# Group 0 of a fused linear layer computed with x stationary, and W1 and W2 loaded over 128 partitions

## The chip, the core and the metric

The kernel runs on one core of a Trainium2 chip. Its time is device time in microseconds, the median of several executions. TensorE multiplies, VectorE (DVE), ScalarE (ACT) and GpSimd (POOL) work on rows in SBUF, and SyncE (SP) issues most of the DMA transfers; ScalarE issues some at the start.

## What is computed

```python
# x (4, 1024, 512), cond (4, 256), W (1536, 512), b (512), all fp32
hidden = concatenate([cond, cond], axis=-1)            # (4, 512)
x_mean = mean(x, axis=1, keepdims=True)                # (4, 1, 512)
fused = concatenate([x, x_mean * ones, hidden * ones], axis=-1)
out = x + relu(einsum('bld,do->blo', fused, W) + b)
```

W falls into W1 (for x), W2 (for the mean) and W3 (for cond), of 512 rows each. The mean and cond parts are the same for all rows of a batch, so they make one bias line for each batch: mean @ W2 + hidden @ W3 + b.

## The kernel before

The 4096 rows of x are 8 groups of 512; two groups make a batch. Only x @ W1 is done for every row. To keep fp32 precision each factor is split in a high part of a shorter float type and a rest (xh and xl, w1h and w1l), and a product takes three matmuls: xh w1h, xl w1h, xh w1l. The inner dimension 512 is four slices k of 128.

In groups 0 to 6 W1 is stationary and x streams: an output tile t (one of four) is 128 output columns by 512 rows, in a PSUM bank of its own (ps_y, four banks). In group 7, the last, x rows are stationary and W1 columns stream (`last_product`), so its output needs no turning back. Group 0 is done in two halves of 256 rows, k outermost, as data arrive.

For a piece of x (one k of one group) VectorE turns it by 32x32 blocks into PSUM (`turn_x`, L331), ScalarE writes xh and adds up the columns for the mean (`x_high`, L257), VectorE subtracts to get xl (`x_low`, L337). x lies in SBUF by quadrants of 32 partitions, one for each 128 columns; a load of a group of x is four transfers of 32 partitions, one a quadrant, with rows of 512 bytes. ScalarE makes w1h (L250), GpSimd w1l (L227). W1 and W2 are loaded by quadrants as well (`load_w1`, `load_w2`), with rows of 2 KB.

Behind a tile, ScalarE adds bias and applies relu (L275), VectorE turns it back (L344), GpSimd adds x (L232), SP stores. The first tiles are complete before their bias is known: ScalarE saves eight of them in relu_t (L262), and applies bias and relu later. The bias of batch b needs both its groups: VectorE forms w2x, the W2 rows weighted by x's sums (`mean_terms`, L356 to L361, 128x512 a step), TensorE adds over partitions (`mean_bias`, L476), VectorE adds the constant part const_row (L411), which comes from cond and W3 (`const_product`, L525), and spreads it (`sum_bias`, L375, L378). The last group takes its bias as a line of rows, stored to DRAM and loaded back (bias_line, last_bias).

Each engine runs its instructions in the order of the code; semaphores alone tie them together. SP's queue is one list: x0, W1, cond, x1, x2, W2, b, x3, W3, x4 to x7, then the last group's x as rows, then the stores. Rows of it stand below, with the change.

Of the kernel before, what the change touches and what calls it, by code (L numbers as in the profile page):

```python
# [37 lines left out]
WARM = 14  # L38


def build(nc, x, cond, w, bvec, out):
# [13 lines left out]
    pieces = [(0, l, HL, k) for l in (0, HL) for k in range(NK)]  # L55
    pieces += [(g, 0, NL, k) for g in range(1, G) for k in range(NK)]

    def pieces_to(g):
        return NK * g + NK * (g > 0 if isinstance(g, int) else 1)
# [24 lines left out]
    bias_line = nc.dram_tensor("bias_line", [D], F32).ap()  # L84
# [7 lines left out]
    with ExitStack() as ctx:  # L92
# [13 lines left out]
        w2x = sb("w2x", [P, D])  # L106
# [10 lines left out]
        xsum = sb("xsum", [P, G + 1, NK])  # L117
# [6 lines left out]
        bias_row = sb("bias_row", [P, P])  # L124
# [53 lines left out]

# [3 lines left out]
        def _(sp):  # L182
# [430 lines left out]
```

## Time and profile before

| | |
|---|---|
| Median of 3 runs | 104.74 us (104.71 to 105.04) |
| Profiled execution, its own time | 105.25 us, of which the span of the core 103.1 us |
| TensorE busy | 97.4 us, 95% of the span |
| VectorE / ScalarE / GpSimd busy | 79% / 46% / 40% |
| DMA | 21.39 MB, mean 207 GB/s |

The durations come from the profiled execution. It has 2.15 us around the span, and is 0.5 us above the median. Matmuls are pipelined, so the time from one start to the next is what a product costs, not the duration in its row. The profile counts a DMA packet for each contiguous run that an engine moves, and small packets of 4 bytes that signal completion.

### The profile page before, as it was taken

How to read it: one execution, taken by the hardware profiler on the slowest of the kernel's cores; microseconds unless marked ns; L12 is line 12 of the kernel's file. 1: busy time of each engine (PE TensorE's matmuls, PEld its weight loads, DVE VectorE, ACT ScalarE, POOL GpSimd, SP SyncE). 2: the span in 40 equal slices, each digit the busy share in tenths (PEclk: the TensorE clock that was granted, in tenths of full speed). 3: DMA queues.
4: the chain of work that ended last, by engine and by line, in shares of the span. 5: the costliest groups of instructions: out<-in, count | busy, mean ns of one | idle time of the engine just before them, and what ended most of it. 6: DMA issues, size and time to landing. Idle time of an engine off the chain costs nothing.

```text
span 103.1 us, 1694 instructions
## 1 busy us (share of the span) xinstructions
PE 97.4 (95%) x523; PEld 78.3 (76%) x523; DVE 81.7 (79%) x146; ACT 47.3 (46%) x116; POOL 41.0 (40%) x37
## 2 busy tenths in 40 slices
PE   5989999999999898999999999999999999999970
PEld 2349999778888585888888886888888886888960
DVE  3173869979879999999999994999999994839660
ACT  3277426875606549777487100874744004610000
POOL 1029700000000000999857700468577059992000
PEclk9999999999999999999999999999999999999997
DMA  2999999999999999999999999300591690199995
GB/s 63 290 306 273 220 214 216 235 235 218 233 270 253 209 224 221 225 225 224 219 296 349 309 282 251 97 0 0 111 267 29 144 253 14 39 279 263 230 330 183
DMA packets 34990, 21.39 MB, mean 207 GB/s; under 512 B 1572, under 2 KB 32680, under 8 KB 34984
## 3 DMA queue, kind: packets, MB, share of 16 engines
q1 hardware_dynamic: 33400, 20.13, 85.4%
q10 hardware_dynamic: 1584, 1.18, 3.8%
q8 instruction: 3, 0.05, 0.2%
q14 instruction: 3, 0.02, 0.1%
HBM read 12.91 MB, written 8.39 MB: 207 GB/s over the span
## 4 chain that ended last, share of the span: by engine, by line
PE 57%; SPq 18%; DMA 10%; DVE 7%; issue 3%; ACT 1%; DVEq 0%
PE ps_y L457 46%; DMA xa<-in_x_dram 10%; SPq L162 9%; PE ps_y L558 4%; PE ps_y L560 4%; PE ps_y L559 4%; SPq L166 2%; SPq L170 2%; DVE w2x L361 2%; DVE ps_xt L331 2%; SPq L158 2%; SPq L195 2%; ACT xh L257 1%; DVE xl L337 1%; SPq L190 1%
## 5 line engine op out<-in xcount | busy, mean ns | idle before, releaser
L232 POOL TENSOR_TENSOR xa<-xa,back 128x512 f32 x28 | 35.6, 1295 | 45.8 <-DVE back L344 45.8
L457 PE MATMUL ps_y<-xh,w1h 128*128 (+2 forms) x128 | 43.7, 368 | 0.3 <-ACT w1h L250 0.3
L457 PE MATMUL ps_y<-xl,w1h 128*128 (+2 forms) x128 | 43.1, 363 | 0.0
L457 PE MATMUL ps_y<-xh,w1l 128*128 (+2 forms) x128 | 42.9, 363 | 0.0
L257 ACT ACTIVATE xh<-ps_xt 128x512 fp32r<-128x512 f32 (+1 forms) x36 | 19.7, 549 | 21.1 <-DVE ps_xt L331 21.1
L331 DVE STREAM_TRANSPOSE ps_xt<-xa 128x512 f32<-128x512 f32 (+1 forms) x36 | 22.3, 643 | 5.8 <-DMA xa<-in_x_dram 5.4
L457 PEld LDWEIGHTS ps_y<-xh,w1h 128*128 128x128 f32 x128 | 22.6, 188 | 5.6 <-issue 0.8
L457 PEld LDWEIGHTS ps_y<-xh,w1l 128*128 128x128 f32 x128 | 22.6, 189 | 3.9
L337 DVE TENSOR_TENSOR xl<-ps_xt,xh 128x512 fp32r<-128x512 f32 (+1 forms) x36 | 22.2, 618 | 4.1 <-ACT xh L257 4.1
L457 PEld LDWEIGHTS ps_y<-xl,w1h 128*128 128x128 f32 x128 | 22.7, 189 | 3.5
L275 ACT ACTIVATE relu_t<-ps_y,bias 128x512 f32<-128x512 f32 x20 | 13.5, 686 | 16.5 <-DVE bias L378 15.0
L344 DVE STREAM_TRANSPOSE back<-relu_t 128x512 f32<-128x512 f32 x28 | 18.6, 685 | 1.1 <-ACT relu_t L275 1.1
L361 DVE SCALAR_TENSOR_TENSOR w2x<-w,bsum,w2x 128x512 f32<-128x512 f32 x12 | 9.0, 751 | 0.4
L227 POOL TENSOR_TENSOR w1l<-w,w1h 128x512 fp32r<-128x512 f32 x4 | 5.1, 1304 | 6.2 <-ACT w1h L250 6.2
L257 ACT ACTIVATION_READ_ACCUMULATOR xh<-ps_xt 128x1 f32 x36 | 7.1, 196 | 0.0
L558 PE MATMUL ps_y<-w1h,xh 128*128 128x512 f32 (+1 forms) x20 | 6.9, 347 | 0.0
L559 PE MATMUL ps_y<-w1l,xh 128*128 128x512 f32 (+1 forms) x20 | 6.9, 346 | 0.0
L560 PE MATMUL ps_y<-w1h,xl 128*128 128x512 f32 (+1 forms) x20 | 6.9, 345 | 0.0
L454 PE MATMUL ps_mean<-warm 128*128 128x512 bf16 x14 | 5.6, 587 | 1.2 <-DVE warm L390 1.2
L275 ACT ACTIVATE relu_t<-relu_t,bias 128x512 f32<-128x512 f32 x8 | 5.0, 710 | 1.7 <-DVE bias L378 1.7
L454 PEld LDWEIGHTS ps_mean<-warm 128*128 128x128 bf16 x14 | 1.9, 141 | 4.4 <-issue 3.2
L262 ACT ACTIVATE relu_t<-ps_y 128x512 f32<-128x512 f32 x8 | 4.5, 596 | 1.2 <-PE ps_y L457 1.2
(34 smaller groups left out, 35.8 us busy)
## 6 DMA issues: line engine op xcount, KB each, us to landing
xa<-in_x_dram SPq DMA_DIRECT2D x28, 256.0 KB, 7.2
out_dram<-xa SPq DMA_DIRECT2D x28, 256.0 KB, 4.1
w<-in_L_cond_W_dram SPq DMA_DIRECT2D x4, 256.0 KB, 7.6
w<-in_L_cond_W_dram SPq DMA_DIRECT2D x2, 512.0 KB, 8.3
w<-in_x_dram SPq DMA_DIRECT2D x4, 256.0 KB, 6.2
out_dram<-w SPq DMA_DIRECT2D x3, 256.0 KB, 3.2
xa<-in_x_dram SPq DMA_DIRECT2D x4, 128.0 KB, 3.6
xa<-in_x_dram ACTq DMA_DIRECT2D x4, 128.0 KB, 4.0
```

What stands on the lines that cost most here:

```text
L162: eng.dma_start(xa[Q * j:Q * j + Q, g], xv[g, j]).then_inc(x_landed[g], 16)
L232: nc.gpsimd.tensor_tensor(rows, rows, back[:, t], ALU.add).then_inc(added, 1)
L257: nc.scalar.activation(xh[:, g % SLOTS, k, l:l + nl], ps_xt[:, n % XT_BANKS, 0:nl], ACT.Copy, accum_out=xsum[:, part, k:k + 1]).then_inc(x ...
L275: nc.scalar.activation(relu_t[:, slot], products, ACT.Relu, bias=bias[:, g // H, t, g // H:g // H + 1]).then_inc(relu_done, 1)
L331: nc.vector.transpose(ps_xt[:, n % XT_BANKS, 0:nl], xa[:, g, l // Q:(l + nl) // Q, Q * k:Q * k + Q]).then_inc(xt_ready, 1)
L337: nc.vector.tensor_tensor(xl[:, g % SLOTS, k, l:l + nl], ps_xt[:, n % XT_BANKS, 0:nl], xh[:, g % SLOTS, k, l:l + nl], ALU.subtract).then_i ...
L344: nc.vector.transpose(back[:, n % BACK_RING], relu_t[:, n % RELU_RING].rearrange("p (lb om) -> p lb om", om=Q)).then_inc(turned_back, 1)
L361: nc.vector.scalar_tensor_tensor(out=w2x[:], in0=w2[:, k], scalar=bsum[:, k:k + 1], in1=w2x[:], op0=ALU.mult, op1=ALU.add).then_inc(w2x_st ...
L457: return nc.tensor.matmul(ps_y[:, t, ls], lhs, rhs, start=start, stop=stop, skip_group_check=True)
L558: nc.tensor.matmul(y, xh[:, slot, k, rows], cols_h, start=start, stop=False, skip_group_check=True)
L559: nc.tensor.matmul(y, xh[:, slot, k, rows], cols_l, start=False, stop=False, skip_group_check=True)
L560: return nc.tensor.matmul(y, xl[:, slot, k, rows], cols_h, start=False, stop=stop, skip_group_check=True)
```

## The change

Group 0 is computed as group 7 is: x rows stationary (128 a tile), W1 columns streaming, 512 wide. Its x comes in three parts, of 128, 128 and 256 rows, and its first 24 products (tiles r = 0, 1) need parts one and two. Its tiles leave PSUM as rows: ScalarE copies them into w1's place (`save_first`), GpSimd adds the bias line there, ScalarE applies relu, GpSimd adds x rows, which are loaded a second time into group 0's place in xa; SP stores them after group 3. The bias line of batch 0 goes through DRAM for that, between the loads of x5, x6 and x7.

W1 is loaded slice by slice over 128 partitions (slice 0 in two transfers of 64 partitions, one from SP and one from ScalarE), W2 in four transfers of 128. VectorE makes half of each slice of w1h. cond is loaded behind x1. VectorE forms batch 1's sums ahead of its wait for W3's product, into a second half of w2x, and TensorE does the mean products of odd batches in ps_const's bank; those of batches 0 and 1 stand in the third and the last tile of group 2. Six tiles are saved for a later relu, not eight. The loops over groups on TensorE and GpSimd are written out. The warm-up has 10 matmuls, not 14.

```diff
-WARM = 14
+WARM = 10
-    pieces = [(0, l, HL, k) for l in (0, HL) for k in range(NK)]
+    PARTS = ((0, P), (P, P), (2 * P, 2 * P))
+    FIRST = ((0, 0), (0, 1), (0, 2), (1, 0), (1, 1), (0, 3), (1, 2), (1, 3)) + tuple((2, k) for k in range(NK))
+    pieces = [(0, *PARTS[part], k) for part, k in FIRST]
...
-        def load_w1(eng, first, end, quadrants):
-            for j in quadrants:
-                eng.dma_start(w1[Q * j:Q * j + Q, first:end], wv[0, j, :, first:end]).then_inc(w1_landed[first], 16)
-
-        def load_w2(eng, quadrants):
-            for j in quadrants:
-                eng.dma_start(w2[Q * j:Q * j + Q], wv[1, j]).then_inc(w2_landed, 16)
+        def load_w1(eng, k, first, end):
+
+            eng.dma_start(w1[Q * first:Q * end, k], wv[0, first:end, :, k]).then_inc(w1_landed[k], 16)
+
+        def load_w2(eng, k):
+            eng.dma_start(w2[:, k], wv[1, :, :, k]).then_inc(w2_landed, 16)
...
+            load_x(sp, 4, ORDER)
+            load_x(sp, 5, ORDER)
+
+            sp.wait_ge(bias_summed, 1)
+            for j in range(NQ):
+                sp.dma_start(bias_line[0, P * j:P * j + P], bias_row[Q * j, 0]).then_inc(bias_stored, 16)
+            load_x(sp, 6, ORDER)
+            sp.wait_ge(bias_stored, 16 * NQ)
+            sp.dma_start(last_bias[:], bias_line[0].partition_broadcast(P)).then_inc(last_bias_landed, 16)
+            load_x(sp, 7, ORDER)
...
+            for n, (g, t) in enumerate(tiles):
+                residual(g, t, n + 1)
+                r = n - BIAS_FROM
+                if 0 <= r < NR:
+
+                    pool.wait_ge(y_free, r + 1)
+                    pool.wait_ge(last_bias_landed, 16)
+                    nc.gpsimd.tensor_tensor(first_y[:, r], first_y[:, r], last_bias[:], ALU.add).then_inc(first_biased, 1)
+                r = n - X0_FROM
+                if 0 <= r < NR:
+
+                    pool.wait_ge(first_relu_done, r + 1)
+                    pool.wait_ge(first_x_landed, 16 * NR)
+                    nc.gpsimd.tensor_tensor(first_x[:, r], first_x[:, r], first_y[:, r], ALU.add).then_inc(first_added, 1)
...
             turn_x(n_x)
             turn_and_split(n_x, n_x + NK)
+            mean_terms(1)
             dve.wait_ge(const_summed, 1)
             dve.wait_ge(b_landed, 16 * NQ)
             nc.vector.tensor_tensor(const_row[:], ps_const[:, 0:P], b_row[:], ALU.add).then_inc(const_ready, 1)
             dve.wait_ge(const_ready, 1)
             sum_bias(0)
-            mean_terms(1)
+            sum_bias(1)
...
+            def first_rows(k, r, x, w, start=False, stop=False):
+
+                return nc.tensor.matmul(ps_y[:, r], x[:, 0, k, P * r:P * r + P], w[:, k], start=start, stop=stop, skip_group_check=True)
```

`wv` is W1 and W2 seen as (s, j, m, k, o), row 128 j + 32 k + m of each: `wv[0, j, :, 0]` is 32 rows one after another, `wv[1, :, :, k]` is 4 blocks of 32 rows, the blocks 128 rows apart.

SP's queue from its start, before; names are target<-source, then partitions x elements, and how many. One DMA row is one kind of transfer (w is w1, w2 or w3 here; ScalarE's queue issues as many of x0 and W1 beside it).

```order
L158 DMA xa<-in_x_dram 32x8x128 x2
L166 DMA w<-in_L_cond_W_dram 32x512 x4
L166 DMA w<-in_L_cond_W_dram 32x2x512 x2
L158 DMA xa<-in_x_dram 32x8x128 x2
L190 DMA cond_c<-in_cond_dram 4x64 [waits cond_zeroed]
L190 DMA cond_c<-in_cond_dram 4x64 x3
L162 DMA xa<-in_x_dram 32x16x128 x8
L170 DMA w<-in_L_cond_W_dram 32x4x512 x4
L195 DMA b_row<-in_L_cond_b_dram 32x128 x4
L162 DMA xa<-in_x_dram 32x16x128 x4
```

The same place in the changed kernel:

```order
L171 DMA xa<-in_x_dram 32x4x128 x2
L179 DMA w<-in_L_cond_W_dram 64x1x512
L171 DMA xa<-in_x_dram 32x4x128 x2
L179 DMA w<-in_L_cond_W_dram 128x1x512 x3
L171 DMA xa<-in_x_dram 32x8x128 x4
L175 DMA xa<-in_x_dram 32x16x128 x4
L211 DMA cond_c<-in_cond_dram 4x64 [waits cond_zeroed]
L211 DMA cond_c<-in_cond_dram 4x64 x3
L175 DMA xa<-in_x_dram 32x16x128 x4
L182 DMA w<-in_L_cond_W_dram 128x1x512 x4
L216 DMA b_row<-in_L_cond_b_dram 32x128 x4
L175 DMA xa<-in_x_dram 32x16x128 x4
```

The W1 and W2 transfers cover 64 or 128 partitions in place of 32, and are fewer; x0 comes in three parts, cond stands behind x1.

VectorE behind the turning of group 3's pieces, before: last splits, constant row, bias 0, sums of batch 1, first tiles turned back.

```order
L337 TENSOR_TENSOR xl<-ps_xt,xh 128x512 [waits xh_ready] x2
L411 TENSOR_TENSOR const_row<-ps_const,b_row 128x128 [waits b_landed,const_summed]
L375 SCALAR_TENSOR_TENSOR bias_row<-ps_mean,const_row 128x128 [waits mean_done,const_ready]
L378 STREAM_TRANSPOSE bias<-bias_row 128x128 [waits bias_summed]
L356 TENSOR_TENSOR bsum<-xsum 128x4 [waits w2x_step,mean_done]
L358 TENSOR_SCALAR w2x<-w,bsum 128x512 [waits bsum_ready]
L361 SCALAR_TENSOR_TENSOR w2x<-w,bsum,w2x 128x512 [waits w2x_step] x3
L344 STREAM_TRANSPOSE back<-relu_t 128x512 [waits relu_done] x2
```

And in the changed kernel:

```order
L407 TENSOR_TENSOR xl<-ps_xt,xh 128x512 [waits xh_ready] x2
L436 TENSOR_TENSOR bsum<-xsum 128x4 [waits w2x_step]
L438 TENSOR_SCALAR w2x<-w,bsum 128x512 [waits bsum_ready]
L441 SCALAR_TENSOR_TENSOR w2x<-w,bsum,w2x 128x512 [waits w2x_step] x3
L517 TENSOR_TENSOR const_row<-ps_const,b_row 128x128 [waits b_landed,const_summed]
L456 SCALAR_TENSOR_TENSOR bias_row<-ps_mean,const_row 128x128 [waits mean_done,const_ready]
L459 STREAM_TRANSPOSE bias<-bias_row 128x128 [waits bias_summed]
L456 SCALAR_TENSOR_TENSOR bias_row<-ps_const,const_row 128x128 [waits mean_done]
L459 STREAM_TRANSPOSE bias<-bias_row 128x128 [waits bias_summed]
L417 STREAM_TRANSPOSE back<-relu_t 128x512 [waits relu_done]
```

The five rows of sums of batch 1 have moved ahead of the wait for const_summed; the first turn back stands behind both biases.

## Rows read from the trace of the kernel before

**Rows 1.** The page: span, and part 1 (busy time and share of the span, instructions).

```profile
span 103.1 us, 1694 instructions
PE 97.4 (95%) x523; PEld 78.3 (76%) x523; DVE 81.7 (79%) x146; ACT 47.3 (46%) x116; POOL 41.0 (40%) x37
```

**Rows 2.** TensorE's timeline: start, us, what, count [idle before, what ended it].

```profile
1.19 5.61 PE L454 MATMUL ps_mean<-warm 128*128 128x512 bf16 x14 [1.19 <-DVE warm L390]
7.07 0.71 PE L457 MATMUL ps_y<-xh,w1h 128*128 128x256 f32 x4 [0.27 <-ACT w1h L250]
...
18.53 0.28 PE L457 MATMUL ps_y<-xh,w1l 128*128 128x256 f32 x1
18.65 0.40 PE L457 MATMUL ps_y<-xh,w1h 128*128 128x512 f32 x1
...
33.66 0.39 PE L457 MATMUL ps_y<-xh,w1l 128*128 128x512 f32 x1
34.52 1.08 PE L525 MATMUL ps_const<-w,cond_t 128*32 128x128 f32 x32 [0.47 <-DMA w<-in_L_cond_W_dram]
...
39.78 0.39 PE L457 MATMUL ps_y<-xh,w1l 128*128 128x512 f32 x1
40.57 0.43 PE L476 MATMUL ps_mean<-w2x,ones 128*32 128x128 f32 x8 [0.40 <-DVE w2x L361]
40.93 0.50 PE L457 MATMUL ps_y<-xh,w1h 128*128 128x512 f32 x1
```

**Rows 3.** The chain that ended last, in order of time: start, us, what.

```profile
36.54 0.29 DVE const_row L411
...
37.42 0.13 DVE bsum L356
...
39.67 0.76 DVE w2x L361
...
41.00 22.01 PE ps_y L457 x96
```

**Rows 4.** The DMA queues from 86.0 to 88.4 us.

```profile
DMA packets 9, 0.01 MB, mean 4 GB/s; under 512 B 4, under 2 KB 8, under 8 KB 8
q1 hardware_dynamic: 8, 0.00, 0.4%
...
bias_line<-bias_row SPq DMA_DIRECT2D x4, 0.5 KB
```

**Rows 5.** The page, DMA packets of the whole span.

```profile
DMA packets 34990, 21.39 MB, mean 207 GB/s; under 512 B 1572, under 2 KB 32680, under 8 KB 34984
```

**Rows 6.** Four stretches: engines' busy time, granted clock, share of DMA engines, GB/s.

```profile
core 0: us, PE busy (x) PEld busy (x) DVE busy (x) ACT busy (x) POOL busy (x), PEclk, DMA share, GB/s
5.00:6.50 1.50, 1.50 (x6) 0.55 (x4) 0.90 (x3) 0.93 (x5) 0.00 (x0) 1.00 1.02 337
7.80:9.80 2.00, 2.00 (x19) 2.00 (x19) 0.77 (x2) 1.65 (x6) 2.00 (x3) 1.00 1.20 292
11.00:14.50 3.50, 3.50 (x32) 3.50 (x31) 2.84 (x8) 1.79 (x8) 1.14 (x1) 1.00 1.21 217
51.80:54.20 2.40, 2.40 (x12) 2.01 (x11) 2.24 (x5) 2.17 (x6) 1.11 (x1) 1.00 1.05 308
```

**Rows 7.** The DMA queues from 100.2 us to the end, in 40 slices.

```profile
GB/s 396 395 396 339 396 452 382 438 353 325 325 353 339 396 339 353 367 339 269 241 226 170 226 169 99 28 28 28 14 14 0 0 0 0 0 0 0 0 0 0
```

**Rows 8.** The timelines of VectorE, ScalarE and GpSimd.

```profile
4.69 0.79 DVE L331 STREAM_TRANSPOSE ps_xt<-xa 128x256 f32<-128x256 f32 x2 [2.89 <-DMA xa<-in_x_dram]
6.30 0.63 ACT L250 ACTIVATE w1h<-w 128x512 fp32r<-128x512 f32 x1
7.09 5.05 POOL L227 TENSOR_TENSOR w1l<-w,w1h 128x512 fp32r<-128x512 f32 x4 [6.20 <-ACT w1h L250]
...
30.91 1.32 DVE L331 STREAM_TRANSPOSE ps_xt<-xa 128x512 f32<-128x512 f32 x2 [0.65 <-DMA xa<-in_x_dram]
...
37.59 5.02 ACT L275 ACTIVATE relu_t<-relu_t,bias 128x512 f32<-128x512 f32 x8 [1.69 <-DVE bias L378]
```

More of the change, by code:

```diff
@@ L105, in build @@
         w3 = sb("w3", [P, 2, CK, D])
-        w2x = sb("w2x", [P, D])
+        w2x = sb("w2x", [P, 2, D])
         ones = sb("ones", [P, Q])
@@ L203, in _ @@
                 sp.dma_start(last_x[:, r], x_rows[LAST, :, r]).then_inc(last_x_landed, 16)
-            for g in range(LAST):
+            for g in range(1, LAST):
                 if g == LAST - 2:
@@ L472, in mean_bias @@
             def mean_bias(b):
+                if b == 1:
+                    pe.wait_ge(const_ready, 1)
+                elif b > 1:
+                    pe.wait_ge(bias_ready, b - 1)
                 pe.wait_ge(w2x_step, NK * b + NK)
                 for j in range(NQ):
-                    last = nc.tensor.matmul(ps_mean[Q * j:Q * j + Q, 0:P], ones[:, 0:Q], w2x[:, P * j:P * j + P], start=True, stop=True)
+                    last = nc.tensor.matmul(mean_bank(b)[Q * j:Q * j + Q, 0:P], ones[:, 0:Q], w2x[:, b % 2, P * j:P * j + P], start=True, stop=True)
@@ new lines, in _ @@
+            for k in range(NK):
+                pe.wait_ge(w1h_ready, k + 1)
+                pe.wait_ge(w1h_rest_ready, k + 1)
+                for r in (0, 1):
+                    piece = FIRST.index((r, k))
+                    pe.wait_ge(xh_ready, piece + 1)
+                    first_rows(k, r, xh, w1h, start=(k == 0))
+                    pe.wait_ge(xl_ready, piece + 1)
+                    first_rows(k, r, xl, w1h)
+                if k == 0:
+                    first_low(0)
+                elif k > 1:
+                    first_low(k - 1)
@@ new lines, in _ @@
+            first_low(NK - 1, stop=True)
+            for k in range(NK):
+                piece = FIRST.index((2, k))
+                pe.wait_ge(xh_ready, piece + 1)
+                if k == NK - 1:
+                    pe.wait_ge(xl_ready, piece + 1)
+                    for r in (2, 3):
+                        first_rows(k, r, xh, w1h)
+                        first_rows(k, r, xl, w1h)
+                        first_rows(k, r, xh, w1l, stop=True).then_inc(y_ready, 1)
+                    break
+                for r in (2, 3):
+                    first_rows(k, r, xh, w1h, start=(k == 0))
+                pe.wait_ge(xl_ready, piece + 1)
+                for r in (2, 3):
+                    first_rows(k, r, xl, w1h)
+                    first_rows(k, r, xh, w1l)
@@ L516, in _ @@
+            pe.wait_ge(y_free, 2)
+            for k in range(NK):
+                pe.wait_ge(xl_ready, pieces_to(1) + k + 1)
+                for t in (0, 1):
+                    last = product(1, k, t)
+                    if k == NK - 1:
+                        last.then_inc(y_ready, 1)
+            for t in (2, 3):
+                pe.wait_ge(y_free, t + 1)
                 tile(1, 1, t)
```

322 lines of the change are left out of this document (183 added, 139 removed).

## The prediction

> **What bounds the kernel now.** I read the page's busy shares first [rows 1]: TensorE is busy 95% of a span of 103.1 us, so the time is TensorE's first product, its work, and its gaps. Its own timeline gives these [rows 2]. Products start at 7.07 us, as w1h becomes ready; group 0 runs to 18.65 us without a gap. From there a 512-column product comes every 0.227 us (33.66 in the row is the last before a stop). Two stops follow, both in group 2. The one ahead of the constant products: 33.66 + 0.23 = 33.89 to 34.52, 0.63 us, for W3. The one ahead of batch 1's mean product: 39.78 + 0.23 = 40.01 to 40.57, 0.56 us, for w2x. From 41.00 the chain that ended last is TensorE's products, 96 of them in one piece of 22.01 us [rows 3].
>
> The chain also shows what set 40.57 [rows 3]. VectorE can start on group 3's x at 30.91, after 0.65 us of waiting for its DMA [rows 8]; I call that the landing. VectorE turns and splits its four pieces, reaches const_row at 36.54, and makes batch 1's w2x from 37.42 to 39.67 + 0.76 = 40.43. So behind group 3's x stand 5.7 us of splitting, then constant and bias, then 3.0 us of sums. Before it in the load queue stand x0 (1 MB), W1 (1 MB), x1, x2, W2: what stretches the loads stretches the kernel.
>
> **How many DMA engines a transfer uses.** This decides the case, and two counts of packets show it. In 86.0 to 88.4 us four transfers of one row store bias_row [rows 4]. The queue has 8 packets, 4 of them under 512 bytes: one data packet and one small completion packet each. Every engine that takes part leaves one completion packet, so each of these used one engine. The whole page has 1572 packets under 512 bytes [rows 5]. The program issues 96 transfers whose outermost count is 32 or 128 on both sides, 4 of cond with outermost count 4 (rows of 256 bytes), and 4 of bias_row with 1. With sixteen engines for the first kind, four for cond, one for bias_row: 96 x 16 + 4 x (4 + 4) + 4 x 1 = 1536 + 32 + 4 = 1572, to the packet. Were cond and bias_row to signal from sixteen engines, it would be 1536 + 80 + 64 = 1680. So a count of 4 outermost means four engines.
>
> The Trainium skill says the same in general: in "DMA: Bandwidth & Descriptors", on why a DMA increments its semaphore by 16, the hardware generator takes the largest number up to 16 that divides the slowest count of source and of destination, and the lowest-numbered engines. By that rule the new W loads, 4 at the source and 128 at the destination, get four engines, and the time is that of my first case below; were it not to hold, it would be that of the second. Trace and rule agree for the counts 1 and 4; no transfer of before has different counts on its two sides, so no run here shows that case yet.
>
> **The change, part by part.**
>
> *W1 and W2 over 128 partitions.* The destination counts 128 partitions, but the source is walked as (j, m, o): outermost 4 with a stride of 128 rows, then 32. For W1's first slice each of two transfers has outermost 2 at the source, 64 at the destination. The unseen price is what happens when the sides differ. Bounds: the destination decides, sixteen engines; or the smaller count decides, four and two engines. I take the smaller: both counts seen so far were obeyed, and a split by outermost index can't make sixteen parts of four.
>
> Then engine 0 carries, ahead of group 3's x: half of slice 0 (64 rows of 2 KB over the two queues), a quarter of slices 1 to 3 (96 rows), a quarter of W2 (128 rows): 288 rows. Beside these its sixteenth of four groups of x, 256 KB or 512 packets of 512 bytes. Rates per engine, from the windows [rows 6]: the W1 stretch moves 337 GB/s, 21 GB/s an engine, 97 ns a row. The x stretch of 7.8 to 9.8 moves 292, 18.3 an engine, 28 ns a packet; from 11.0 on x moves at 217, 13.6 an engine, 38 ns. The start of flow: x0's first half is in at 4.69 [rows 8], 0.52 MB at 292 GB/s is 1.8 us, so 2.9. Middle case: 2.9 + 288 x 0.091 + 512 x 0.028 = 2.9 + 26.2 + 14.3 = 43.4 us for group 3's x, against 30.9. Here 0.091 lies between those 97 ns and the 83 ns of the fastest stretch there is, the last stores at 396 GB/s, 24.8 an engine [rows 7]; few engines share the memory, so I lean to neither. Lower bound 2.9 + 288 x 0.083 + 14.3 = 41.1; upper, with W at 97 ns and x at 38, 2.9 + 27.9 + 19.5 = 50.3.
>
> The start: slice 0 is in at 2.9 + 0.9 (x's first 128 rows) + 64 x 0.091 = 9.6, and w1h's half 0.4 later: first product about 10.0 instead of 7.07. Slice 3 is in at 9.6 + 0.9 + 96 x 0.091 = 19.2, its w1l 0.4 + 1.3 later (GpSimd needs 5.05 us for four [rows 8]), so rows 0 and 1 of group 0 end near 21.3 where all of group 0 ended at 18.65. The rest of x0 is in at 21.0; VectorE and ScalarE need some 5 us for its pieces and the two copies between them, so group 0 ends near 27.3, group 1 near 39, and TensorE comes to batch 1's mean product near 50.
>
> *Products 512 wide.* Group 0 had 96 products of 256 columns in 18.65 - 7.07 = 11.58 us; now 48 of 512 at 0.227, 10.9 us. A saving of 0.7 us of TensorE that only counts if it isn't waiting.
>
> *Batch 1's sums ahead of W3, its mean product in the middle of the last tile.* At the same landing L of group 3's x: const_ready is L + 5.7 + 3.0 + 0.35 = L + 9.1; then mean product 0.36 and its restart 0.11, then six products 1.36: group 3 starts at L + 11.0. Before, it started at 40.93 + 0.11 + 12 x 0.227 = 43.8, L + 12.9. This part is worth 1.9 us. const_product, a tile later than before, then doesn't wait for W3 (34.52 before).
>
> *Group 0's own path* (copies to w1's place, four adds of bias and four of x on GpSimd, four relu on ScalarE, 1 MB more loads): hidden. GpSimd works 1.3 us a tile where TensorE needs 2.75, and is idle most of the second half; if bias 0 were late on its line, GpSimd's adds would hold turned_back, and ScalarE's relu behind it. Relu is the near thing: before, eight saved tiles took 5.02 us from 37.59 [rows 8]; now six are saved, and three x steps stand among their relus, each behind VectorE's turn of that piece, so bank 2 comes free some 6.4 us after bias_ready (const_ready + 0.65). TensorE wants it 5.45 us after group 3's start (const_ready + 1.9): 7.05 against 7.35, a margin of 0.3 us. Without it TensorE would wait by as much as relu is late. The shorter warm-up costs nothing where it ends (1.19 + 10 x 0.43 = 5.5) before any product could start. TensorE then idles from 5.5 to 10, and its products may run at the warm-up's pace for a while (0.43 us per 512 columns, the 1.2 GHz level, against 0.227 later): 11 or 12 of group 0's products so slowed are 2.4 us. TensorE has about that to spare, since it comes to the mean product near 50 and const_ready stands at 43.4 + 9.1 = 52.5, so this too is put at nothing; its upper end, 1 us, lies inside the range.
>
> *The loop written out* costs no time that a row shows.
>
> **Sum.** L moves 43.4 - 30.9 = +12.5, the order gives -1.9: +10.6 us on 105.25 us of the profiled execution (0.5 above the median), so 115.8; on the median 104.74, 115.3. After group 3's start nothing changes the 56 us left.
>
> **The rivals.**
> (1) Forecast: W on two and four engines, 0.63. L = 41.1 gives 104.74 + 10.2 - 1.9 = 113.0, L = 50.3 gives 122.2. Its own range is 112.5 to 121: x at 38 ns all the way is what sixteen busy engines get, and most of them will stand idle. For it speak the packet counts; against it, that no row shows a transfer whose sides differ.
> (2) The other side: W over sixteen engines, 0.30. For it: the destination has 128 partitions, and a sixteen-fold split of it is possible. Against: the source has no sixteenth. Then slice 0 is in before 5 us, products start at about 5.5, group 0 ends near 17.7, and the order's 1.9 us is gained, with up to 0.4 more if W2, at 308 instead of 217 GB/s, lets group 3's x come 1.4 us sooner (VectorE is busy with batch 0's sums until 30.91 - 0.65 = 30.3): 102.4 to 102.9, I say 102.7. It decides against me as soon as slice 0 lands before 6 us.
> (3) Sixteen engines, but the relu margin or the bias line on the load queue fails, 0.07: bank 2 late by 1 to 2 us, or x6 behind the wait on bias_summed; 103.5 to 106.
>
> **Numbers.** Less than 0.3% is no change that a measurement of this kernel can tell. Slower: 0.63 of (1) and 0.02 of (3); same 0.03; faster 0.30 + 0.02. Since cases on both sides hold 93% of the chance, the range has to take in both: 102.3 to 120; beside it the likeliest one's own, 112.5 to 121.
>
> **What would show it.** The page's packets under 512 bytes: each W transfer that uses four engines leaves 12 completion packets fewer. ScalarE's first wait for W1 ends at 9 to 10 us (right) or before 5 (wrong). VectorE's first turn of group 3 at 41 to 50 or at 29 to 31. A wait of TensorE ahead of batch 1's mean product; group 3 starting 11.0 us after that turn. If relu's margin fails, TensorE waits for ScalarE 5.5 us into group 3. The forecast is wrong above all if sides that differ are split by the destination.

## The result

Side by side, the kernel before takes 104.89 us (median of 4 runs, 104.71 to 105.09) and the changed kernel 125.34 us (4 runs, 124.95 to 125.73): a ratio of 1.196, interval 1.193 to 1.200. That is slower, as the forecast's likeliest case said, but by 20.5 us instead of 10.6, and beyond the range. The profiled execution took 125.53 us, its span 123.7. Some executions of any of these kernels fall into a slower state, and every median and ratio here and below leaves them out.

The page of the changed kernel: span and busy shares, the granted clock in 40 slices of 3.1 us, and the packets.

```profile
span 123.7 us, 1487 instructions
PE 101.3 (82%) x471; PEld 78.4 (63%) x471; DVE 84.3 (68%) x155; ACT 48.0 (39%) x126; POOL 46.1 (37%) x41
...
PEclk9995559999999999555899999999999999999999
...
DMA packets 34024, 22.71 MB, mean 184 GB/s; under 512 B 1497, under 2 KB 30561, under 8 KB 34017
```

TensorE works hardly longer than before (101.3 against 97.4 us busy), but in a span 20.6 us longer [rows 1]; its granted clock falls twice to half (1.2 GHz), from 9 to 19 us and from 50 to 60; in the page of before no such slice stands. The packets settle the number of engines. With sixteen engines for every W transfer (first experiment below) a page of this program has 1720 packets under 512 bytes. Taking away the 16 completions of each of its 16 W transfers, and adding 2 x 2 for the two-engine transfers and 7 x 4 for the others, gives 1720 - 256 + 32 = 1496; the page has 1497. So W1 and W2 went over two and four engines.

VectorE's timeline, the instructions that waited for a load (start, us, what, in brackets the idle time before and the load): three slices of w1h, x0's second half, x1, batch 0's sums behind W2, and group 3's x.

```profile
12.43 0.29 DVE L479 CAST w1h<-w 128x256 fp32r<-128x256 f32 x1 [8.33 <-DMA w<-in_L_cond_W_dram]
...
17.76 0.29 DVE L479 CAST w1h<-w 128x256 fp32r<-128x256 f32 x1 [0.78 <-DMA w<-in_L_cond_W_dram]
...
21.41 0.29 DVE L479 CAST w1h<-w 128x256 fp32r<-128x256 f32 x1 [3.16 <-DMA w<-in_L_cond_W_dram]
...
22.92 0.79 DVE L401 STREAM_TRANSPOSE ps_xt<-xa 128x256 f32<-128x256 f32 x2 [1.02 <-DMA xa<-in_x_dram]
...
27.26 1.32 DVE L401 STREAM_TRANSPOSE ps_xt<-xa 128x512 f32<-128x512 f32 x2 [0.60 <-DMA xa<-in_x_dram]
...
44.17 0.17 DVE L436 TENSOR_TENSOR bsum<-xsum 128x4 f32<-128x4 f32 x1 [5.18 <-DMA w<-in_L_cond_W_dram]
...
50.15 1.32 DVE L401 STREAM_TRANSPOSE ps_xt<-xa 128x512 f32<-128x512 f32 x2 [2.93 <-DMA xa<-in_x_dram]
```

Group 3's x can be turned at 50.15 against 30.91 before [rows 8]: 19.2 us later. Four stretches of the changed kernel show how the loads run:

```profile
core 0: us, PE busy (x) PEld busy (x) DVE busy (x) ACT busy (x) POOL busy (x), PEclk, DMA share, GB/s
5.00:12.00 7.00, 0.55 (x2) 0.00 (x0) 0.00 (x0) 0.00 (x0) 0.00 (x0) 0.77 0.33 109
12.00:20.00 8.00, 6.03 (x15) 4.42 (x16) 3.96 (x16) 3.44 (x17) 3.83 (x3) 0.56 0.54 160
32.00:45.00 13.00, 13.00 (x59) 10.77 (x58) 7.13 (x16) 5.03 (x14) 0.00 (x0) 1.00 0.53 151
45.00:54.50 9.50, 2.56 (x12) 1.78 (x10) 6.27 (x10) 2.50 (x8) 0.00 (x0) 0.75 1.06 218
```

From 5 to 20 us only a third to a half of the engines' time is used, and 0.53 while W2 comes in (32 to 45), where the stretches read from before have 1.02 to 1.21 at 217 to 337 GB/s [rows 6]. TensorE's timeline shows the price:

```profile
1.19 4.37 PE L561 MATMUL ps_mean<-warm 128*128 128x512 bf16 x10 [1.19 <-DVE warm L471]
...
12.90 0.79 PE L593 MATMUL ps_y<-w1h,xh 128*128 128x512 f32 x1 [7.35 <-ACT w1h L297]
...
47.17 0.39 PE L564 MATMUL ps_y<-xh,w1l 128*128 128x512 f32 x1
54.66 1.94 PE L655 MATMUL ps_const<-w,cond_t 128*32 128x128 f32 x32 [7.10 <-DMA w<-in_L_cond_W_dram]
56.33 0.69 PE L587 MATMUL ps_mean<-w2x,ones 128*32 128x128 f32 x8
56.95 0.79 PE L564 MATMUL ps_y<-xh,w1h 128*128 128x512 f32 x1
...
61.27 0.43 PE L587 MATMUL ps_const<-w2x,ones 128*32 128x128 f32 x8
...
83.22 0.43 PE L587 MATMUL ps_mean<-w2x,ones 128*32 128x128 f32 x8 [0.20 <-DVE w2x L441]
...
87.14 0.50 PE L564 MATMUL ps_y<-xh,w1h 128*128 128x512 f32 x1 [1.24 <-ACT relu_t L330]
```

The first product is at 12.90 (7.07 before [rows 2]). Group 3 starts 1.8 us after the mean product at 61.27, at 63.1, against 43.8. Two more waits, 0.20 us at 83.22 and 1.24 at 87.14, were not in the forecast. VectorE's sums, for batch 1 (w2x in 2.8 us) and for batch 2 (w2x in 4.7 us):

```profile
55.78 0.15 DVE L436 TENSOR_TENSOR bsum<-xsum 128x4 f32<-128x4 f32 x1
55.97 0.49 DVE L438 TENSOR_SCALAR w2x<-w,bsum 128x512 f32<-128x512 f32 x1
56.49 2.33 DVE L441 SCALAR_TENSOR_TENSOR w2x<-w,bsum,w2x 128x512 f32<-128x512 f32 x3
58.74 0.28 DVE L517 TENSOR_TENSOR const_row<-ps_const,b_row 128x128 f32<-128x128 f32 x1
...
77.18 1.09 DVE L436 TENSOR_TENSOR bsum<-xsum 128x4 f32<-128x4 f32 x1
78.31 1.47 DVE L438 TENSOR_SCALAR w2x<-w,bsum 128x512 f32<-128x512 f32 x1
79.82 3.25 DVE L441 SCALAR_TENSOR_TENSOR w2x<-w,bsum,w2x 128x512 f32<-128x512 f32 x3
```

### The profile page after: what moved, and what is told of

It reads as the page before. It is cut to its first block, busy times and chain, and to the rows that moved or that the text cites. A ratio compares the mean times of both kernels' runs of the same rounds, so it can differ in the third digit from the quotient of the medians.

```text
span 123.7 us, 1487 instructions
## 1 busy us (share of the span) xinstructions
PE 101.3 (82%) x471; PEld 78.4 (63%) x471; DVE 84.3 (68%) x155; ACT 48.0 (39%) x126; POOL 46.1 (37%) x41
## 2 busy tenths in 40 slices
DMA packets 34024, 22.71 MB, mean 184 GB/s; under 512 B 1497, under 2 KB 30561, under 8 KB 34017
## 4 chain that ended last, share of the span: by engine, by line
SPq 34%; PE 33%; DVE 16%; DMA 8%; issue 4%; ACT 1%; DVEq 0%; ACTq 0%
PE ps_y L564 22%; SPq L175 13%; DMA w<-in_L_cond_W_dram 8%; SPq L171 8%; DVE xl L407 4%; SPq L216 4%; DVE ps_xt L401 4%; DVE back L417 4%; SPq L179 3%; SPq L182 3%; PE ps_y L688 3%; PE ps_y L690 3%; PE ps_y L689 3%; DVE w2x L441 2%; PE ps_const L655 2%
## 5 line engine op out<-in xcount | busy, mean ns | idle before, releaser
L270 POOL TENSOR_TENSOR xa<-xa,back 128x512 f32<-128x512 f32 x24 | 30.6, 1292 | 50.4 <-DVE back L417 50.3
L564 PE MATMUL ps_y<-xh,w1h 128*128 128x512 f32 x96 | 38.7, 403 | 1.2 <-ACT relu_t L330 1.2
L564 PE MATMUL ps_y<-xl,w1h 128*128 128x512 f32 x96 | 37.9, 395 | 0.0
L564 PE MATMUL ps_y<-xh,w1l 128*128 128x512 f32 x96 | 37.8, 394 | 0.0
L304 ACT ACTIVATE xh<-ps_xt 128x512 fp32r<-128x512 f32 (+2 forms) x40 | 20.5, 512 | 32.8 <-DVE ps_xt L401 32.6
L401 DVE STREAM_TRANSPOSE ps_xt<-xa 128x512 f32<-128x512 f32 (+2 forms) x40 | 23.0, 596 | 7.7 <-DMA xa<-in_x_dram 7.3
L407 DVE TENSOR_TENSOR xl<-ps_xt,xh 128x512 fp32r<-128x512 f32 (+2 forms) x40 | 22.7, 569 | 2.4 <-ACT xh L304 2.4
L564 PEld LDWEIGHTS ps_y<-xh,w1l 128*128 128x128 f32 x96 | 18.3, 191 | 3.9
L330 ACT ACTIVATE relu_t<-ps_y,bias 128x512 f32<-128x512 f32 x18 | 12.2, 690 | 10.4 <-DVE bias L459 9.5
L593 PE MATMUL ps_y<-w1h,xh 128*128 128x512 f32 x16 | 7.4, 492 | 9.9 <-ACT w1h L297 8.8
L593 PE MATMUL ps_y<-w1h,xl 128*128 128x512 f32 x16 | 7.2, 451 | 0.0
```

Of the source, the lines that this page charges most:

```text
L270: nc.gpsimd.tensor_tensor(rows, rows, back[:, t], ALU.add).then_inc(added, 1)
L304: nc.scalar.activation(xh[:, g % SLOTS, k, l:l + nl], ps_xt[:, n % XT_BANKS, 0:nl], ACT.Copy, accum_out=xsum[:, part, k:k + 1]).then_inc(x ...
L330: nc.scalar.activation(relu_t[:, slot], products, ACT.Relu, bias=bias[:, g // H, t, g // H:g // H + 1]).then_inc(relu_done if n < SAVED el ...
L401: nc.vector.transpose(ps_xt[:, n % XT_BANKS, 0:nl], xa[:, g, l // Q:(l + nl) // Q, Q * k:Q * k + Q]).then_inc(xt_ready, 1)
L407: nc.vector.tensor_tensor(xl[:, g % SLOTS, k, l:l + nl], ps_xt[:, n % XT_BANKS, 0:nl], xh[:, g % SLOTS, k, l:l + nl], ALU.subtract).then_i ...
L564: return nc.tensor.matmul(ps_y[:, t, ls], lhs, rhs, start=start, stop=stop, skip_group_check=True)
```

## The experiments

All times are medians, ratios are against the kernel before on the same chip, with a 95% interval. The chips differ from experiment to experiment, so small differences between experiments are best read from the ratios.

### 1. W by quadrants in the changed kernel (e1)

```diff
-            eng.dma_start(w1[Q * first:Q * end, k], wv[0, first:end, :, k]).then_inc(w1_landed[k], 16)
+            for j in quadrants:
+                eng.dma_start(w1[Q * j:Q * j + Q, first:end], wv[0, j, :, first:end]).then_inc(w1_landed[first], 16)
...
-            eng.dma_start(w2[:, k], wv[1, :, :, k]).then_inc(w2_landed, 16)
+            eng.dma_start(w2[Q * j:Q * j + Q], wv[1, j]).then_inc(w2_landed, 16)
```

The calls and wait counts change with them; slices 2 and 3 come in one transfer for each quadrant, and from slice 1 on all are handed out by SP.

> The changed kernel, with W1 and W2 loaded again by quadrants of 32 partitions (outermost count 32 on both sides); all else as changed. Theory A (the narrow W transfers are the whole loss): packets under 512 bytes go back to sixteen completion packets a transfer, first product near 5.5 us, group 0 ends by 18 us, x of group 3 is in at 30 to 31 us, time 102.4 to 103.5 us. Theory B (part of the 20 us comes from the rest of the change: group 0's path on GpSimd and ScalarE, relu's margin, batch 2's bias): time stays above 105 us.

Measured: 106.27 us (105.81 to 106.77), ratio 1.011 (1.004 to 1.017). So the shape of the W loads is 19.1 of the 20.5 us, and the rest of the change loses 1.2 us where it should have gained 2. VectorE's timeline of this run, its first slice of w1h, x1, group 3's x, and then batch 2's sums:

```profile
4.74 0.29 DVE L479 CAST w1h<-w 128x256 fp32r<-128x256 f32 x1 [0.68 <-DMA w<-in_L_cond_W_dram]
...
17.03 1.32 DVE L401 STREAM_TRANSPOSE ps_xt<-xa 128x512 f32<-128x512 f32 x2 [0.88 <-DMA xa<-in_x_dram]
...
32.28 1.32 DVE L401 STREAM_TRANSPOSE ps_xt<-xa 128x512 f32<-128x512 f32 x2 [0.37 <-DMA xa<-in_x_dram]
...
57.91 1.08 DVE L436 TENSOR_TENSOR bsum<-xsum 128x4 f32<-128x4 f32 x1
59.03 1.48 DVE L438 TENSOR_SCALAR w2x<-w,bsum 128x512 f32<-128x512 f32 x1
60.54 3.24 DVE L441 SCALAR_TENSOR_TENSOR w2x<-w,bsum,w2x 128x512 f32<-128x512 f32 x3
```

The first slice is in at 4.74 instead of 12.43, group 3's x at 32.28 instead of 50.15 (30.91 before: this version hands the quadrants out one after another). Group 3 starts at 43.25, 0.5 us earlier than before. But TensorE then stops twice where the kernel before doesn't:

```profile
63.93 0.43 PE L587 MATMUL ps_mean<-w2x,ones 128*32 128x128 f32 x8 [0.79 <-DVE w2x L441]
...
67.85 0.50 PE L564 MATMUL ps_y<-xh,w1h 128*128 128x512 f32 x1 [1.24 <-ACT relu_t L330]
```

Behind both stands VectorE's sum for batch 2, 5.8 us from 57.91 on, while in the kernel before it took 0.99, 0.48 and 2.32 us for the same three rows. What GpSimd does at that time, group 0's bias adds (L279) between the residual adds (L270):

```profile
57.66 1.31 POOL L279 TENSOR_TENSOR w<-w,last_bias 128x512 f32<-128x512 f32 x1
58.92 1.31 POOL L270 TENSOR_TENSOR xa<-xa,back 128x512 f32<-128x512 f32 x1
60.16 1.50 POOL L279 TENSOR_TENSOR w<-w,last_bias 128x512 f32<-128x512 f32 x1
```

### 2 to 4. Only W1, only W2, and the W loads alone in the kernel before (e2, e3, e4)

e2 has e1's first piece of the diff, e3 its second, and e4 is the kernel before with the changed kernel's W loads:

```diff
+        def load_w1(eng, k, first, end):
+            eng.dma_start(w1[Q * first:Q * end, k], wv[0, first:end, :, k]).then_inc(w1_landed[k], 16)
...
+        def load_w2(eng, k):
+            eng.dma_start(w2[:, k], wv[1, :, :, k]).then_inc(w2_landed, 16)
```

> The changed kernel, with W1 alone by quadrants; W2 still in four transfers with outermost count 4 at the source. Theory A: W2 puts 128 rows of 2 KB on each of four engines where 32 fell on each of sixteen; at the 105 ns a row that the changed kernel showed for it this is 13.4 us in place of 4.7, so x of group 3 is in near 39 to 40 us, and the time is 111 to 114 us. Theory B (W1 carries the loss, W2 hides behind products): below 106 us.

> The changed kernel, with W2 alone by quadrants; W1 still narrow. Theory A: first product near 13 us and group 0's end near 29.6 us stay; x of group 3 is in near 41 us, const_row near 50; TensorE, 11 us late from group 0 on, comes to batch 1's mean product near 50 as well, so the time is 114 to 117 us. Theory B (the W3 and W2 waits carry the loss): below 110 us.

> The kernel before with the W1 and W2 loads of the changed one and nothing else. Theory A: it is slow by about what the changed kernel loses and what the rest of it gains, so 125 to 129 us. Theory B: under 120 us.

Measured: e2, with W1 by quadrants, 114.05 us (1.084, 1.075 to 1.093); e3, with W2 by quadrants, 116.07 (1.104, 1.098 to 1.109); e4, with nothing changed but the loads, 124.76 (1.183, 1.174 to 1.192). Each is what its theory A said, to 0.3 us. Against e1 the narrow W2 costs 7.8 us, the narrow W1 9.8, together 17.6 of the 19.1: they nearly add up. e4 is only 0.6 us below the changed kernel, so the rest of the change gained nothing beside the narrow loads. The count of packets under 512 bytes in e4 is 1348, which is 1572 - 256 + 32 to the packet.

### 5 and 6. GpSimd's adds for group 0 later; W1 on two queues ahead of x0's second part (e5, e6)

e5 is e1 with

```diff
-    BIAS_FROM, RELU_FROM, X0_FROM = 4, 9, 9
+    BIAS_FROM, RELU_FROM, X0_FROM = 8, 14, 16
...
-                if g == LAST - 4:
+                if g == LAST - 2:
```

> The run with W1 and W2 by quadrants again, with three numbers changed: GpSimd adds the bias line to group 0's rows after tiles 8 to 11 (was 4 to 7), ScalarE's relus follow from tile 14 (was 9), GpSimd's adds of x0 from tile 16 (was 9), and group 0's rows are stored after group 5 (was 3). Theory A, GpSimd's adds of two arrays from SBUF hold up VectorE's sums for batch 2: those took 5.8 us there (bsum 1.08, w2x 1.48 and 3.24) beside GpSimd's adds and 3.8 us in the kernel before (0.99, 0.48, 2.32) with one add beside them. They shrink to at most 3.9 us, mean_bias(2) waits for nothing, the wait for batch 2's bias at group 5's start falls from 1.4 us to under 0.3, and the time from 106.27 to 104.0 to 104.8. Rival B, the order of the sums' steps on VectorE makes them late whatever GpSimd does: the sums keep over 5 us or the waits stay, and the time is within 0.5 us of 106.27.

Measured: 109.61 us (109.58 to 111.08), 1.056 (1.040 to 1.072). The mechanism was right and the time wrong. VectorE's sums for batch 2 fall to 3.7 us:

```profile
57.41 0.88 DVE L436 TENSOR_TENSOR bsum<-xsum 128x4 f32<-128x4 f32 x1
58.33 0.48 DVE L438 TENSOR_SCALAR w2x<-w,bsum 128x512 f32<-128x512 f32 x1
58.85 2.32 DVE L441 SCALAR_TENSOR_TENSOR w2x<-w,bsum,w2x 128x512 f32<-128x512 f32 x3
```

TensorE runs from group 1 to the end without a wait, its mean product for batch 3 at 84.7 instead of 87.1. But GpSimd's adds of x0 now stand among the last groups' adds, and its last four begin at 91.31:

```profile
81.32 1.29 POOL L270 TENSOR_TENSOR xa<-xa,back 128x512 f32<-128x512 f32 x1 [3.60 <-DVE back L417]
...
91.31 5.94 POOL L270 TENSOR_TENSOR xa<-xa,back 128x512 f32<-128x512 f32 x4
```

They end at 97.25; the stores of group 6 go out behind them, and the last store lands at 107.0. A second chain is as long as TensorE's: VectorE's turns, GpSimd's last adds, the last nine stores.

e6 is e5 with

```diff
+            load_w1(sp, 1, 2, LOW)
+            load_w1(sp, 2, NK, LOW)
             load_x0(sp, 1, LOW)
...
-            load_w1(sp, 1, 2, ORDER)
-            load_w1(sp, 2, NK, ORDER)
...
+            load_w1(act, 1, 2, HIGH)
+            load_w1(act, 2, NK, HIGH)
```

> The run before this one in the list, and every slice of W1 handed out on two queues at once, quadrants 0 and 1 on SP and 2 and 3 on ACT, ahead of group 0's second part, as the kernel before does. Theory A, the serial hand-out was why everything landed 1.4 us later than before (x3 at 32.3 against 30.9): x3 lands by 31.2, group 3 starts near 42.0 (before 43.8), and the time is 102.3 to 103.6, under the kernel before. Rival B, the loads are bound by the bytes: x3 lands at 32 or later and the time is within 0.4 us of the run before this one.

Measured: 112.21 us, 1.077 (1.067 to 1.088). Both were wrong. Group 3's x is in at 29.8, earlier than in the kernel before, as theory A had it, but x0's second part, now behind all of W1, is in only at 8.73 (VectorE waits 1.97 us for it) and holds group 0 back: TensorE stands 2.55 us ahead of 9.51 and works at half clock to 14.7, so batch 1's mean product comes 3.0 us later than in e5. Whether the four transfers that ScalarE hands out in addition also cost time, this run doesn't separate.

### 7 to 9. What put group 3's start 13.0 us behind its x, not 11.0 (e7, e8, e9)

All three are the changed kernel with one edit each.

```diff
-                    elif t == 2 and k == NK // 2:
+                    elif t == 3 and k == 1:
                         const_product()
                         mean_bias(0)
```

> The changed kernel with narrow W loads, and the product of cond and W3 with batch 0's mean product moved from tile 2 of group 2 (k = 2) to tile 3 (k = 1). Theory A, W3's landing (54.5) came last ahead of group 3, 2 us behind the chain of x3's landing: TensorE does 9 products more before it waits, group 3 starts 1.5 to 2.2 us earlier (from 63.1 to about 61.1) and the time falls from 125.3 to 123.1 to 123.8. Rival B, the chain behind x3 alone sets group 3's start: the time stays within 0.4 us of 125.3.

```diff
-WARM = 10
+WARM = 44
```

> The changed kernel with 44 warm-up matmuls in the place of 10, so that TensorE is busy up to the first product at 12.9. Theory A, the half clock of the first products (0.427 us each from 12.9 to 19) is hidden, since the third and fourth slices of W1 land at 17.7 and 21.4 and group 0's end hangs on the fourth: the first products take 0.22 us, group 0 ends within 0.5 us of 29.6, and the time is within 0.4 us of 125.3. Rival B, the missing warm-up costs what its slow products cost: 1 to 2.5 us faster than 125.3.

```diff
+                for _n in range(33):
+                    nc.tensor.matmul(ps_mean[:], warm[:, 0:P], warm[:], start=True, stop=True)
                 pe.wait_ge(cond_spread, 1)
                 pe.wait_ge(w3_landed, 16 * 2)
```

> The changed kernel with narrow W loads, and 33 idle matmuls of 0.21 us ahead of TensorE's wait for W3 (they do no part of the computation), so that TensorE does not stand still for the 7.3 us ahead of the product of cond and W3. Theory A, after the wait it is the half clock (0.427 us a product, 54.7 to 60) that puts group 3's start 2 us behind what the chain from x3's landing allows: group 3 starts at 60.6 to 61.4 (was 63.1) and the time is 123.0 to 124.0. Rival B, the clock is nothing and W3's landing is what came last: the start stays at 63 and the time within 0.5 us of 125.3.

Measured: e7 124.02 us, ratio 1.192 (1.178 to 1.206); e8 124.77, 1.194 (1.182 to 1.207); e9 123.76, 1.179 (1.172 to 1.186). e7 and e8 miss their theory A's range by 0.2 us, e9 lies in it; no rival B is met. In e8 the first products take 0.23 us and batch 1's mean product comes at 61.39 as it did at 61.27: the slow start is hidden, and the 0.6 us that it is below 125.3 lies within the spread of its runs (124.2 to 126.0). In e7 TensorE has 9 products less to do after the wait, and const_row ends the wait of batch 1's mean product at 58.12. Group 3 starts at 61.44, and its x could be turned at 49.21: 12.2 us behind it instead of 13.0, since the six products between still take 0.43 us each. In e9, TensorE's mean products for batches 0 and 1:

```profile
54.73 0.40 PE L587 MATMUL ps_mean<-w2x,ones 128*32 128x128 f32 x8
...
58.09 0.43 PE L587 MATMUL ps_const<-w2x,ones 128*32 128x128 f32 x8
```

With the idle matmuls the products between take 0.23 us (granted clock 1.00 from 53.8 to 60, where the changed kernel has 0.50 from 54.6 to 60), and group 3 starts at 59.94, 10.8 us behind the turn of its x (49.16), as the prediction's own sum had it (11.0). Of the 3.2 us by which it starts earlier 1.0 are the load's, and 2.2 come with the clock. TensorE's last product comes 2.4 us earlier (118.23 against 120.63) and not 3.2, since batch 2's mean product then waits 1.00 us for its sums instead of 0.20; the median falls by 1.6. So the clock alone accounts for all that group 3 was late against the sum, with the products still behind W3. e7, at the low clock, has 0.7 us of it back. The two gains overlap and aren't to be added.

### 10 to 12. GpSimd's adds spread; slice 1 on two queues; the sums put back (e10, e11, e12)

e10 is e1 with

```diff
-    BIAS_FROM, RELU_FROM, X0_FROM = 4, 9, 9
+    BIAS_AT, RELU_AT, X0_AT = (4, 5, 8, 9), (10, 11, 12, 13), (10, 11, 12, 13)
```

e11 is e10 with

```diff
-            load_w1(sp, 1, 2, ORDER)
+            load_w1(sp, 1, 2, LOW)
...
             load_x0(act, 1, HIGH)
+            load_w1(act, 1, 2, HIGH)
```

and e12 is e10 with

```diff
-            mean_terms(1)
             dve.wait_ge(const_summed, 1)
...
             sum_bias(0)
-            sum_bias(1)
+            mean_terms(1)
...
+                if n == 1:
+                    sum_bias(1)
...
+                            if g == H + 1 and k == 3:
+                                mean_bias(1)
```

> The run with W1 and W2 by quadrants, with GpSimd's bias adds for group 0 after tiles 4, 5, 8 and 9 (were 4 to 7), and ScalarE's relus and GpSimd's adds of x0 after tiles 10 to 13 (were 9 to 12), so that fewer of GpSimd's adds stand beside VectorE's sums for batch 2; group 0's rows are stored after group 3 again. Theory A, with the sums at under 4.8 us TensorE waits for nothing between group 1's start and the last group, as in the run with all adds later, and the stores aren't pushed to the end: 103.3 to 104.4, 1.9 to 2.9 us below 106.27. Rival B, whatever moves GpSimd's adds later ends in later stores: 105.5 or more.

> The run before this one in the list, with slice 1 of W1 handed out on two queues (quadrants 2 and 3 on ScalarE's, behind group 0's second part). Theory A, TensorE is the bound and its start decides: slice 1 and those behind it land about 1 us earlier, TensorE's stops in group 0 (1.3 us at slice 2) shrink by 0.5 to 1 us, and the time is 0.3 to 1.0 us under the run before. Rival B, ScalarE's two more hand-outs delay its first high half and the first product by 0.9 us: within 0.3 us of the run before, or slower.

> The run with GpSimd's adds spread (second in the list), with batch 1's sums put back behind batch 0's: VectorE makes them after batch 0's bias, TensorE's mean product for batch 1 stands in group 3's first tile (k = 3), and its bias is summed after the turn of tile 0. Theory A, with group 0's own path the relu that needs batch 1's bias comes two tiles later, and TensorE is continuous either way: within 0.4 us of the run with GpSimd's adds spread. Rival B, the step of the prediction, group 3 waits for the sums: 1.5 to 2.2 us slower than it.

Measured: e10 106.47 us, 1.014 (1.007 to 1.020); e11 104.90, 0.999 (0.993 to 1.005); e12 106.93, 1.019 (1.013 to 1.024). e10 has batch 3's mean product 2 us earlier than e1 (85.2 against 87.1) and is no faster: rival B's time. Its sums for batch 3 now stand beside GpSimd's moved adds and take 5.4 us (e5's take 3.5), and GpSimd's last add ends at 94.84, as e1's does at 94.94:

```profile
78.17 2.63 DVE L436 TENSOR_TENSOR bsum<-xsum 128x4 f32<-128x4 f32 x1
...
84.38 10.46 POOL L270 TENSOR_TENSOR xa<-xa,back 128x512 f32<-128x512 f32 x8 [3.60 <-DVE back L417]
```

e11 is 1.6 us below e10, more than theory A's 0.3 to 1.0, and level with the kernel before. e12 is 0.5 us above e10, with intervals that overlap, near theory A's 0.4 and far from rival B's 1.5 to 2.2: with group 0's rows out of the chain of relus, batch 1's sums can stand early or late. In e11 all eight residual adds of the last two groups run back to back:

```profile
82.70 10.47 POOL L270 TENSOR_TENSOR xa<-xa,back 128x512 f32<-128x512 f32 x8 [2.82 <-DVE back L418]
```

### 13. Without GpSimd's eight adds for group 0 (e13)

e11 with both adds of GpSimd for group 0 taken out, and the waits on them turned to ScalarE's relu and the loads.

```diff
-                    nc.gpsimd.tensor_tensor(first_y[:, r], first_y[:, r], last_bias[:], ALU.add).then_inc(first_biased, 1)
...
-                    nc.gpsimd.tensor_tensor(first_x[:, r], first_x[:, r], first_y[:, r], ALU.add).then_inc(first_added, 1)
```

> The run with slice 1 of W1 on two queues and GpSimd's adds spread, with GpSimd's eight adds for group 0 left out (its rows are stored without bias and without x0; the loads, ScalarE's relus and the stores stay). Theory A, what the faster loads and the sums ahead of W3 gain is eaten by GpSimd's eight more adds (10.4 us of them), beside VectorE's sums for batches 2 and 3 and ahead of the last eight adds of the groups, behind which the last stores stand: VectorE's sums take 3.8 us and less, GpSimd's last add ends 1 to 2 us earlier than 93.2, and the time is 102.3 to 103.8. Rival B, the end is bound by TensorE and the stores alone: within 0.5 us of 104.9.

Measured: 103.57 us (103.15 to 104.54), 0.985 (0.980 to 0.991). Theory A's time: 1.3 us below e11. The sums take 3.7 us for batches 2 and 3. GpSimd's last adds in its profiled execution come in two pieces with a rest between, no longer one block:

```profile
82.35 5.01 POOL L271 TENSOR_TENSOR xa<-xa,back 128x512 f32<-128x512 f32 x4 [3.60 <-DVE back L408]
87.96 5.04 POOL L271 TENSOR_TENSOR xa<-xa,back 128x512 f32<-128x512 f32 x4 [0.60 <-DVE back L408]
```

The end of the last add, 93.0, is no earlier than e11's 93.2, in an execution that was 1 us above its median; that piece of the expectation isn't borne out by this trace, and neither does it show where the 1.3 us were saved (TensorE's last product is at 99.42, e11's at 98.29).

### 14. The moved sums alone, in the kernel before (e14)

```diff
+            mean_terms(1)
             dve.wait_ge(const_summed, 1)
...
-            mean_terms(1)
+            sum_bias(1)
...
-                    elif t == 1 and k == NK // 2:
+                    elif t == 2 and k == NK // 2:
                         const_product()
                         mean_bias(0)
+                    elif t == 3 and k == NK // 2:
+                        mean_bias(1)
```

> The kernel before with one part of the change alone: the sums for batch 1 ahead of W3's product (a second half of w2x, batch 1's mean product in the bank of the product of cond and W3), the product of cond and W3 in tile 2 of group 2 and batch 1's mean product in tile 3. Theory A, TensorE's two stops there are all there is to gain (0.86 us ahead of the product of cond and W3 at 34.52 and 0.79 at 40.57, less 0.2 to 0.3 that such a step takes without a wait): group 3 starts 0.9 to 1.2 us earlier than 43.8, and 0.5 to 1.2 us of it is left in the time. Rival B, the step of the prediction: 1.9 us less. Rival C, the last stores and GpSimd's last adds set the end: within 0.3 us of before.

Measured: 108.81 us (107.85 to 109.44), 1.040 (1.036 to 1.044): slower, against all three. TensorE is ready for group 3 at 43.5, and then waits for a free bank. ScalarE's relus of the eight saved tiles, and TensorE's wait:

```profile
40.16 5.02 ACT L283 ACTIVATE relu_t<-relu_t,bias 128x512 f32<-128x512 f32 x8 [4.65 <-DVE bias L389]
```

```profile
46.16 0.49 PE L467 MATMUL ps_y<-xh,w1h 128*128 x1 [2.52 <-ACT relu_t L283]
```

Batch 0's bias is now made behind batch 1's sums, so these relus begin at 40.16 instead of 37.59 [rows 8] and take 5.02 us; the bank of group 3's first tile is free one relu behind them. So group 3 starts 2.4 us later than before; the runs lie 2.9 to 4.5 us above before's median, and what the rest of that is, I can't name. With group 0 out of that queue of relus (e10 against e12) the moved sums cost nothing: the two parts of the change belong together.

## Why the prediction was wrong

**Right.** The rule of the engines: two and four, from the smaller count at the source, shown by packets (1497 for 1496, 1348 for 1348). With it the direction, and that the W loads outweigh all the rest (19.1 us in e1, 19.7 in e4). The Trainium skill's rule, in "DMA: Bandwidth & Descriptors", the section on why a DMA increments its semaphore by 16, agrees for sides that differ too, the case that no row of before showed. The sums behind a landing L: const_row begins at 58.74 = 50.15 + 8.6 (forecast: ready at L + 9.1, it ends at + 8.9). The hidden warm-up: e8. The loads' order W1, W2 in one queue: e2 and e3 nearly add up.

**The step that failed first** is the size of L, "Middle case: 2.9 + 288 x 0.091 + 512 x 0.028 = 2.9 + 26.2 + 14.3 = 43.4 us". It was 50.15, inside the step's own bounds (50.3). Per row of W an engine took (12.43 - 3.6) / 64 = 138 ns in the first slice, (21.41 - 17.76) / 32 = 114 in the fourth and (44.17 - 31.9) / 128 = 96 in W2 (31.9 is when the last transfer of group 2's x, just ahead of it in the queue, landed). That is 30.1 us in all instead of 26.2. The rest, 17.1 us instead of 14.3, is x's: a packet took (27.26 - 22.92) / 128 = 34 ns in x1 and (50.15 - 44.17) / 128 = 47 in x3, not 28. I had argued that x is faster where most engines stand idle. That was wrong: engine 0 has as many packets of x as before, and while x3 came the engines didn't stand idle (DMA share 1.06 from 45 to 54.5 us). I also had left this upper bound's 122.2 out of a range that ended at 120. The first slice is slowest, with slices 1 to 3 and x0's parts handed out around it on two queues; why a row takes 138 ns there and 96 in W2, I didn't test.

**"const_product, a tile later than before, then doesn't wait for W3"** failed by 7.1 us: I moved L and not W3, which stands behind it in the same queue. What that cost was 2 us, and it came through the next step: **"this too is put at nothing; its upper end, 1 us"**, the clock. I looked for it at the start, where e8 shows it hidden; it cost where I had not looked, after the wait for W3, where TensorE's products took 0.43 us until 60. e9 gives the whole 2.2 us back, e7, with W3 off the path but the clock low, 0.7.

**"This part is worth 1.9 us"** compared landings, but TensorE itself was the bound of the kernel before: its two stops there add up to 1.2 us [rows 2], and no more could be had there. With fast loads (e1) it got 0.5 us with the load 1.4 us later; with the part taken out again (e12) the loss was 0.5 us, within the spread; alone (e14) it lost 3.9 us.

**"hidden", group 0's own path, and "After group 3's start nothing changes"** failed together. GpSimd's adds stand beside VectorE's sums: 5.8 us in e1 instead of the 3.8 of before, and 3.7 in e5 and e13. So batch 2's bias is late and TensorE stops, 1.24 us ahead of 87.14 in the changed kernel. I had priced GpSimd by its own idle time, and the relu's margin 20 us too early, at batch 1's bias, where it held. The Trainium skill has the mechanism: "SBUF — State Buffer", the section on who interferes with whom, says that a VectorE instruction with two inputs in SBUF contends with a GpSimd one that reads SBUF, that a tensor_scalar can contend in a mode that takes both ports, and that whoever issues first has the shared ports for the whole instruction. e1's rows agree: a sum of four columns (two inputs) takes 1.08 us, where batch 1's took 0.15 in the changed kernel with GpSimd at rest, w2x's last three steps 3.24 instead of 2.32, and the first product, a tensor_scalar, 1 us more than its 0.48. No run shows which mode that one was in. Rival (3) named the place and not the cause.

**The sum by what was measured:** L +19.2, the order +0.1 instead of -1.9 (63.1 - 50.15 against 43.8 - 30.9), later waits +1.7 with what a restart takes: 21.0, and TensorE's last product does stand 21.1 us later (120.63 against 99.50). The end follows 0.5 us closer behind it: 20.6, the difference of the spans.

**Why no version beats both kernels.** e11, the best complete one, is level with before. Its TensorE ends 1.2 us earlier (98.3 against 99.5), but GpSimd's last add (93.2 against 93.5) and the span (103.0 against 103.1) hardly do. e13, which leaves out GpSimd's eight adds, has 1.5% less than before; so these adds are about what group 0's new path costs, though the trace of e13 doesn't show the way by which. What a path for group 0 that doesn't need GpSimd would give was not tried.

## What to carry over

Count, for each transfer, the slowest dimension on both sides before joining four transfers into one: a gathered view whose outermost count is 4 uses four engines, and what stands behind it in the queue waits for those four. When a landing moves, move all landings behind it too, and look at the clock after every new long wait. An idle engine isn't free if its instructions read SBUF beside those of the engine that feeds the path; and an order that costs nothing with one part of a change can lose 4% without it.

## What was not expected of the hardware

- Where a slice of W1 goes over two engines, a row of 2 KB takes 138 ns, in W2 over four engines 96, and with all sixteen busy 97 [rows 6]. Fewer engines at work didn't make each faster.
- After 7.1 us without work TensorE's 32 small products took 1.94 us instead of 1.08 [rows 2], and the next products 0.43 instead of 0.227 us until 60 us, at a granted clock of 0.50. 33 idle matmuls in the wait kept it at 1.00 (e9).
- Beside GpSimd's adds a VectorE product of w2x takes 1.48 us instead of 0.48, and a sum of 4 columns 1.08 instead of 0.15; in e10 one took 2.63.
- e5 ended TensorE's work 2.2 us earlier than e1 (99.19 against 101.36) and was 3.3 us slower: its last nine stores need 9 to 10 us behind GpSimd's last add (97.25 to 107.0), at 0.86 of the DMA engines' time.
